# A graph network's edge bucketing: source and destination packed into one 16-bit value, shorter sums, slot rows written in two halves

## What is computed

```python
def _layernorm(x, axis=-1, eps=1e-05):
    m = jnp.mean(x, axis=axis, keepdims=True)
    v = jnp.var(x, axis=axis, keepdims=True)
    return (x - m) / jnp.sqrt(v + eps)
...
# layer 0: attention over the edges; each edge (rows, cols) = (src, dst)
def _L0_gnn_ref(embeds, qW, kW, vW, rows, cols):
    q = (embeds[rows] @ qW).reshape(e, HEADS, dh)
    k = (embeds[cols] @ kW).reshape(e, HEADS, dh)
    v = (embeds[cols] @ vW).reshape(e, HEADS, dh)
    scores = jnp.clip(jnp.einsum('ehd,ehd->eh', q, k), -10.0, 10.0)
    exp_s = jnp.exp(scores)
    norms = jax.ops.segment_sum(exp_s, rows, num_segments=nvar)[rows]
    w = exp_s / (norms + 1e-08)
    res = jax.ops.segment_sum(w[:, :, None] * v, rows, num_segments=nvar).reshape(nvar, d)
    return embeds + res
...
h = jnp.maximum(_layernorm(x, axis=-1), 0.0)
x = x + _L0_gnn_ref(h, L0_gnn_qW, L0_gnn_kW, L0_gnn_vW, src, dst)
h = jnp.maximum(_layernorm(x, axis=-1), 0.0)
x = x + _L1_gnn_ref(h, src, dst, L1_gnn_W, L1_gnn_b)      # softmax-weighted sum over incoming edges, linear
h = jnp.maximum(_layernorm(x, axis=-1), 0.0)
x = x + _L2_gnn_ref(h, edge_index)                        # ten normalized propagation steps
h = jnp.maximum(_layernorm(x, axis=-1), 0.0)
x = x + _L3_gnn_ref(h, edge_index, L3_gnn_W1, L3_gnn_b1, L3_gnn_W2, L3_gnn_b2)  # two graph convolutions
return x
```

## Time and profile before

| | us |
|---|---|
| median of 3 runs | 4279.61 |
| the profiled execution | 4284.03 |
| its span, first to last instruction | 4282.7 |
| bucketing loop, from the first `bt` to the last copy of placed values | 61.96 to 310.2 |
| from there to the landing of the first row load of attention | 310.2 to 329.8 |
| busy over the whole span: TensorE / VectorE / ScalarE / GpSimd | 3994 / 1952 / 1447 / 602 |

### The profile page before, as it was taken

The page is one execution under the profiler, slowest core; times in us unless marked ns, Lnnn a source line. Parts: engine busy times, 40 slices in busy tenths (PEclk is TensorE's granted clock), DMA queues, the critical chain, the costliest instruction groups (busy, mean ns, idle before and its releaser), DMA issues.

```text
span 4282.7 us, 126097 instructions
## 1 busy us (share of the span) xinstructions
PE 3994.3 (93%) x46462; PEld 3761.0 (88%) x46462; DVE 1951.5 (46%) x4496; ACT 1446.9 (34%) x4588; POOL 601.5 (14%) x707
## 2 busy tenths in 40 slices
PE   2668999999997999899999999999999999979898
PEld 2558999999995556699999999999999999979898
DVE  8998999999997233322222222222222222251211
ACT  1226777777776010122222222222222222221100
POOL 1004656665652000000000000000000000000000
PEclk9778999999998999999999999999999999989899
DMA  1004455455454333256566565655565556546574
GB/s 38 2 4 148 157 169 168 153 173 164 153 172 147 108 112 104 106 202 204 202 202 203 202 204 202 204 201 204 200 205 201 204 200 205 199 147 207 163 214 138
DMA packets 304056, 705.71 MB, mean 165 GB/s; under 512 B 32571, under 2 KB 228539, under 8 KB 303928
## 3 DMA queue, kind: packets, MB, share of 16 engines
q1 hardware_dynamic: 299542, 703.17, 50.6%
q10 hardware_dynamic: 4386, 0.73, 0.1%
HBM read 620.51 MB, written 83.32 MB: 164 GB/s over the span
## 4 chain that ended last, share of the span: by engine, by line
PE 74%; DVE 11%; issue 6%; POOL 4%; DMA 2%; ACT 1%; DVEq 0%; SPq 0%; ACTq 0%; POOLq 0%
PE sum L1544 46%; PE sum L1289 14%; PE sum3a L1289 4%; PE pk L1059 3%; POOL sc L1011 2%; PE pr L1081 2%; POOL wv L1016 2%; DVE onerank L738 1%; DMA rows<-slot_rows_d 1%; DVE qk L935 1%; PE pq L1071 1%; DVE sc L942 1%; DVE hd L983 1%; DVE hT L954 1%; DVE bt L701 1%
## 5 line engine op out<-in xcount | busy, mean ns | idle before, releaser
L1544 PE MATMUL sum<-y,ring 128*128 128x192 f16 x12005 | 993.9, 246 | 4.9 <-ACT y L1446 4.9
L1544 PEld LDWEIGHTS sum<-y,ring 128*128 128x128 fp8e4 x12005 | 992.8, 98 | 5.4 <-issue 5.1
L1544 PE MATMUL sum<-u2b,ring 128*128 128x192 f16 x12005 | 991.2, 246 | 0.0
L1544 PEld LDWEIGHTS sum<-u2b,ring 128*128 128x128 fp8e4 x12005 | 990.5, 98 | 0.0
L1289 PE MATMUL sum<-u,ring 128*128 128x385 f16 (+1 forms) x4802 | 613.0, 288 | 31.1 <-ACT u L1414 22.2
L1552 DVE TENSOR_TENSOR z<-lo,sum 128x96 f32<-128x96 f32 x490 | 124.8, 255 | 1118.8 <-ACT lo L1567 1117.9
L1289 PEld LDWEIGHTS sum<-u,ring 128*128 128x128 fp8e4 x4802 | 435.7, 98 | 198.9 <-issue 36.7
L1059 PE MATMUL pk<-kv,hT 128*128 128x192 f16 x4900 | 488.3, 247 | 22.6 <-DVE hT L954 15.8
L1059 PEld LDWEIGHTS pk<-kv,hT 128*128 128x128 f16 x4900 | 408.8, 99 | 30.6 <-DVE hT L954 15.2
L1144 ACT ACTIVATE kvs<-pk 128x384 f32<-128x384 f32 x735 | 309.0, 437 | 204.9 <-PE pk L1059 139.9
L1567 ACT ACTIVATE lo<-sum 128x96 f32<-128x96 f32 x490 | 123.2, 251 | 745.7 <-PE sum L1544 745.7
(11 more groups left out here) (247 smaller groups left out, 3693.1 us busy)
## 6 DMA issues: line engine op xcount, KB each, us to landing
ring<-adjacency_t SPq DMA_DIRECT2D x490, 800.0 KB, 4.3
ring<-adjacency SPq DMA_DIRECT2D x147, 896.0 KB, 5.0
rows<-slot_rows_d SPq DMA_DIRECT2D x245, 320.0 KB, 6.4
adjacency<-row SPq DMA_DIRECT2D x49, 800.0 KB, 3.4
adjacency_t<-col SPq DMA_DIRECT2D x49, 800.0 KB, 6.0
out_dram<-X SPq DMA_DIRECT2D x6, 336.0 KB
slot_rows_d<-slot_rows SPq DMA_DIRECT2D x4, 156.2 KB
ed<-in_dst_dram ACTq DMA_DIRECT2D x25, 18.0 KB, 1.6
```

What stands on the lines that cost most here:

```text
L1544: m = pe.matmul(ps[r][:, 0:2 * D], w[:, t // 2, :, t % 2], U[:, t, 0:2 * D], start=t == 0, stop=t == TILES - 1)
```

## The change

Source place (0 to 127) and destination place (0 to 255) of an edge go into one 16-bit word, read as bfloat16: the source in the low 7 bits, where its fraction lies, 64 plus the destination's low 7 bits in the exponent, and the destination's eighth bit as the sign (`code`). A product with the one-hot matrix and a sum over zeros keep such a value as it is, so one `vals` of 49 columns takes the place of two. `same2`, `same4` and `prod4` are no longer made: `tensor_rank` adds 36 rows of `same`, which is now in two buffers, the 49th tile, and 24 columns of `prod2`. After the loop VectorE takes the bits apart again in two halves of the tiles (24 and 26), in uint16, into values in float16 that are transposed; ScalarE issues two of the first half's four row writes, SP the others, and the second half's four. Only the first half's are waited for at the end of bucketing; the second half's before attention loads its fifth chunk. The planes of `slots` are uint16 with other codes for the high part, and `hT` is compared with numbers that begin at 64 for the destination (`dpid`, one more iota on GpSimd at the start). ScalarE computes one exponent at the end of bucketing (`warm`). The diff, cut to its core:

```diff
+FIRST_D = 64
+HALF_X = 12
...
+        code = k.buf(ctx, "code", [P, GROUPS, RUN], U16)
...
-        vals = [k.buf(ctx, f"vals{i}", [P, TWOS_RUN, 2, TILES, 2], BF16) for i in range(2)]
+        vals = [k.buf(ctx, f"vals{i}", [P, TWOS_RUN, TILES, 2], BF16) for i in range(2)]
...
-        prod4 = k.buf(ctx, "prod4", [P, TWOS_RUN, EVEN // 4, 2], BF16)
-        same = k.buf(ctx, "sameb", [P, 2, TWOS_RUN, RUN], BF16)
-        same2 = k.buf(ctx, "same2", [P, TWOS_RUN, RUN], BF16)
-        same4 = k.buf(ctx, "same4", [P, RUN // 4, RUN], BF16)
+        same = [k.buf(ctx, f"sameb{i}", [P, 2 * TWOS_RUN, RUN], BF16) for i in range(2)]
...
+        placed = k.buf(ctx, "placed", [P, BTILES, GROUPS], BF16)
+        rows16 = k.buf(ctx, "rows16", [P, 2, BTILES, GROUPS], F16)
+        identh = k.buf(ctx, "identh", [P, P], F16)
+        warm = k.buf(ctx, "warm", [P, 1], F32)
...
+        x_halves = ((0, HALF_X), (HALF_X, PAIRS))
+        pt = [projection.turned[:].bitcast(F16)] + [projection.out[:, i, :].bitcast(F16) for i in range(2)]
...
+            v.tensor_copy(identh[:], k.ident[:])
+            v.memset(placed[:, TILES:BTILES, :], 0.0)
             v.wait_ge(k.base1.sem, k.base1.at(2))
             v.tensor_tensor(rel[:], k.ed[:], over(base[:], RUN), ALU.subtract).then_inc(k.prepared.sem, 1)
             v.tensor_scalar(ti[:], k.es[:], 7, None, ALU.logical_shift_right).then_inc(k.prepared.sem, 1)
+            v.tensor_scalar(half_d, k.ed[:], P, 8, ALU.bitwise_and, ALU.logical_shift_left)
             projection.roots()
             v.wait_ge(k.prepared.sem, k.prepared.at(1))
             v.tensor_scalar(valid[:], rel[:], float(GROUP - 1), None, ALU.is_le).then_inc(k.prepared.sem, 1)
-            v.tensor_scalar(dloc[:], rel[:], 1.0, None, ALU.add)
+            v.tensor_scalar(lower, k.ed[:], P - 1, 7, ALU.bitwise_and, ALU.logical_shift_left).then_inc(k.prepared.sem, 1)
             v.wait_ge(k.prepared.sem, k.prepared.at(3))
             v.scalar_tensor_tensor(valid[:], rel[:], 0.0, valid[:], ALU.is_ge, ALU.mult).then_inc(k.prepared.sem, 1)
+            v.wait_ge(k.prepared.sem, k.prepared.at(2))
+            v.tensor_scalar(k.es[:], k.es[:], P - 1, None, ALU.bitwise_and).then_inc(k.prepared.sem, 1)
             projection.units()
-            v.wait_ge(k.prepared.sem, k.prepared.at(4))
+            v.wait_ge(k.prepared.sem, k.prepared.at(6))
             v.scalar_tensor_tensor(tile1, ti[:], 1.0, valid[:], ALU.add, ALU.mult).then_inc(k.prepared.sem, 1)
-            v.wait_ge(k.prepared.sem, k.prepared.at(5))
-            v.tensor_scalar(ti[:], k.es[:], P - 1, None, ALU.bitwise_and).then_inc(k.prepared.sem, 1)
+            v.scalar_tensor_tensor(lower, lower, float(FIRST_D * P), k.es[:], ALU.add, ALU.add).then_inc(k.prepared.sem, 1)
+            v.wait_ge(k.prepared.sem, k.prepared.at(7))
             v.tensor_copy(tile_odd[:, :, 0:2 * RUN - 1], tile0[:, :, 1:2 * RUN]).then_inc(k.prepared.sem, 1)
-            v.wait_ge(k.prepared.sem, k.prepared.at(6))
-            v.tensor_scalar(sloc[:], ti[:], 1.0, None, ALU.add).then_inc(k.prepared.sem, 1)
             v.wait_ge(k.prepared.sem, k.prepared.at(8))
+            v.tensor_tensor(code[:], lower, half_d, ALU.add).then_inc(k.prepared.sem, 1)
+            v.wait_ge(k.prepared.sem, k.prepared.at(10))
...
+            for h, (x0, x1) in enumerate(x_halves):
+                t = slice(2 * x0, 2 * x1)
+                bits = placed[:, t, :].bitcast(U16)
+                v.tensor_scalar(filled[:, t, :], bits, 0.5, None, ALU.is_gt, ALU.add,
+                                accum_out=k.full[:, h:h + 1]).then_inc(k.full_s.sem, 1)
+                v.tensor_scalar(place[:, t, :], bits, P - 1, None, ALU.bitwise_and).then_inc(k.codes.sem, 1)
+                v.tensor_scalar(second[:, t, :], bits, 2.0 ** 15 - 0.5, 256.0, ALU.is_gt, ALU.mult).then_inc(k.codes.sem, 1)
+                v.tensor_scalar(exponent[:, t, :], bits, 7, None, ALU.logical_shift_right).then_inc(k.codes.sem, 1)
+                v.wait_ge(k.full_s.sem, k.full_s.at(h + 1))
+                v.wait_ge(k.codes.sem, k.codes.at(3 * h + 1))
+                v.scalar_tensor_tensor(rows16[:, 0, t, :], place[:, t, :], 1.0, filled[:, t, :], ALU.add,
+                                       ALU.mult).then_inc(k.decoded.sem, 1)
+                v.wait_ge(k.codes.sem, k.codes.at(3 * h + 3))
+                v.scalar_tensor_tensor(rows16[:, 1, t, :], second[:, t, :], -0.5, exponent[:, t, :], ALU.mult,
+                                       ALU.add).then_inc(k.decoded.sem, 1)
+            bits = placed[:].bitcast(U16)
+            v.scalar_tensor_tensor(k.slots[:, 0, :, :], place, 1.0, filled[:], ALU.add, ALU.mult).then_inc(k.planes.sem, 1)
+            v.tensor_scalar(k.slots[:, 2, :, :], second[:], 1.0, None, ALU.max).then_inc(k.planes.sem, 1)
+            v.tensor_scalar(k.slots[:, 1, :, :], bits, 11, HIGH_D - 1, ALU.logical_shift_right,
+                            ALU.bitwise_and).then_inc(k.planes.sem, 1)
+            v.tensor_scalar(k.slots[:, 3, :, :], bits, 7, LOW_D - 1, ALU.logical_shift_right,
+                            ALU.bitwise_and).then_inc(k.planes.sem, 1)
             v.wait_ge(k.full_ps.sem, k.full_ps.at(1))
-            v.tensor_copy(k.filled[:], pc[0:1, 0:1]).then_inc(k.filled_s.sem, 1)
+            v.tensor_reduce(k.filled[:], pc[0:1, 0:2], AX.X, ALU.add).then_inc(k.filled_s.sem, 1)
...
+            if g >= 2:
+                v.wait_ge(k.ranked.sem, k.ranked.at(g - 1))
             for odd, t in enumerate((tile0, tile_odd)):
-                v.tensor_tensor(same[:, odd, :, :], under(tile1[:, g, :], TWOS_RUN), moved(t, g),
-                                ALU.is_equal).then_inc(k.same.sem, 1)
+                v.tensor_tensor(same[i][:, odd * TWOS_RUN:(odd + 1) * TWOS_RUN, :], under(tile1[:, g, :], TWOS_RUN),
+                                moved(t, g), ALU.is_equal).then_inc(k.same.sem, 1)
             v.wait_ge(k.bt.sem, k.bt.at(g + 1))
             if g >= 2:
                 v.wait_ge(k.placed.sem, k.placed.at(g - 1))
-            v.tensor_tensor(vals[i][:, :, 0, :, :], bt[i][:], of_group(sloc, g), ALU.mult).then_inc(k.sval.sem, 1)
-            v.wait_ge(k.same.sem, k.same.at(4 * g + 2))
-            v.tensor_tensor(same2[:], same[:, 0, :, :], same[:, 1, :, :], ALU.add).then_inc(k.same.sem, 1)
-            v.tensor_tensor(vals[i][:, :, 1, :, :], bt[i][:], of_group(dloc, g), ALU.mult).then_inc(k.dval.sem, 1)
-            v.wait_ge(k.same.sem, k.same.at(4 * g + 3))
-            if g:
-                v.wait_ge(k.ranked.sem, k.ranked.at(g))
-            v.tensor_tensor(same4[:], same2[:, 0:RUN // 4, :], same2[:, RUN // 4:, :], ALU.add).then_inc(k.same.sem, 1)
+            v.tensor_tensor(vals[i][:], bt[i][:], of_group(code[:].bitcast(BF16), g), ALU.mult).then_inc(k.val.sem, 1)
...
-            v.wait_ge(k.prod.sem, k.prod.at(3 * g + 2))
-            v.tensor_tensor(prod4[:], prod2[:, :, 0:EVEN // 4, :], prod2[:, :, EVEN // 4:, :], ALU.add).then_inc(k.prod.sem, 1)
...
-            pe.wait_ge(k.slots_out.sem, k.slots_out.at(GROUPS))
-            for n in range(2 * PAIRS):
-                i, x = divmod(n, PAIRS)
+            for n, (h, i, x) in enumerate((h, i, x) for h, (x0, x1) in enumerate(x_halves) for i in range(2)
+                                          for x in range(x0, x1)):
+                if n in (0, 2 * HALF_X):
+                    pe.wait_ge(k.decoded.sem, k.decoded.at(2 * h + 2))
                 if n >= 24 and n % 8 == 0:
                     pe.wait_ge(k.rows_sb.sem, k.rows_sb.at(n // 8 - 2))
                 pe.transpose(pt[n // 8 % 3][0:2 * GROUPS, (n % 8) * P:(n % 8 + 1) * P],
-                             flat(k.slots[:, i, 2 * x:2 * x + 2, :]), k.identb[:]).then_inc(k.rows_t.sem, 1)
-            pe.wait_ge(k.full_s.sem, k.full_s.at(1))
-            pe.matmul(pc[0:1, 0:1], k.ones[:, 0:1], k.full[:], start=True, stop=True).then_inc(k.full_ps.sem, 1)
+                             flat(rows16[:, i, 2 * x:2 * x + 2, :]), identh[:]).then_inc(k.rows_t.sem, 1)
+            pe.wait_ge(k.full_s.sem, k.full_s.at(2))
+            pe.matmul(pc[0:1, 0:2], k.ones[:, 0:1], k.full[:], start=True, stop=True).then_inc(k.full_ps.sem, 1)
...
-            parts = [same4[:, j, :].rearrange("p (a t) -> p a t", t=2) for j in range(RUN // 4)]
-            parts += [prod[:, :, j, :] for j in range(EVEN, TILES)] + [prod4[:, :, j, :] for j in range(EVEN // 4)]
+            parts = [same[g % 2][:, j, :].rearrange("p (a t) -> p a t", t=2) for j in range(RUN)]
+            parts += [prod[:, :, j, :] for j in range(EVEN, TILES)] + [prod2[:, :, j, :] for j in range(EVEN // 2)]
...
-                t = pe.matmul(po[:, 0:2 * TILES], onerank[:, r // 2, :, r % 2],
-                              vals[g % 2][:, r // 2, :, :, r % 2].rearrange("p i k -> p (i k)"), start=r == 0, stop=r == RUN - 1)
+                t = pe.matmul(po[:, 0:TILES], onerank[:, r // 2, :, r % 2], vals[g % 2][:, r // 2, :, r % 2],
```

(59 more changed lines are left out.)

53 lines of the change are left out of this document (19 added, 34 removed).

## The result

The kernel after took 4226.98 us in the median of 4 runs (4226.25 to 4227.45), the kernel before 4279.34 in 4 runs beside it (4278.96 to 4280.45): a ratio of 0.9877, interval 0.986 to 0.9894, or 52.4 us less. The forecast was 4230.7, in a range of 4224 to 4246. The profiled execution of after took 4226.87, at the median of its runs; that of before took 4284.03, 4.4 above its own.

What follows compares the result with a forecast made beforehand. VectorE was taken to bound the bucketing loop. Codes +2.0, loop -48.0, slot rows in halves -1.6 and exp table -1.3 sum to -48.9 us, from 4279.6 to 4230.7, range 4224 to 4246.

Steps and rivals of the forecast that it cites:

- likeliest case: Whole kernel: bucketing turns of 7.7 to 8.05 us, giving 4226 to 4237 us; chance 0.69.
- Preparation: Ahead of the bucketing loop: making the codes adds 2.0 us on VectorE, bounds +1.4 to +3.
- First and last turn: Bucketing loop's ends: first turn 3.0 us shorter, last turn 0.6 longer as no VectorE bucketing work hides rank.
- placing: Behind the last turn: 12 placing matmuls of half the width and a copy of 49 elements save 1.0 us.
- The turn: Bucketing loop: a turn falls from 9.80 to 7.86 us, 44.6 us less over 23 turns.
- Rank: TensorE in each bucketing turn: 61 matmuls instead of 22, 2.10 us at low clock, 1.86 at high.
- Codes and halves: Between bucketing and attention: 3.0 us of decoding, then slot rows written in halves; net -1.6 us, bounds +2 and -3.5.
- Exp table: Start of attention: loading the table earlier, while slot rows are written, saves the load's 1.28 us, counted as -1.3.
- Attention: Attention's 49 copies of uint16 slots, 100 elements each: 0 us more, bound 2.5.
- (a): Bucketing loop: TensorE takes over the turn, 8.2 to 8.6 us each, total 4238 to 4248 us; chance 0.26.
- (b): Bucketing loop: the burst of 61 rank matmuls becomes the bound, making the kernel slower, 4294 us; chance 0.02.
- (c): Bucketing loop: VectorE's saving moves into waits on `before` or ScalarE's copies, total 4271 to 4288 us; chance 0.02.

Runs made afterwards that it cites:

- 85 rank matmuls: The kernel after with `prod2` not made either, its sums left to TensorE: 4215.96 us, ratio 0.9849 to the kernel before.
- one run: The kernel before with the early exponent alone added: 4277.10 us, ratio 0.9989 to the kernel before.
- the other: The kernel after with a copy in place of the early exponent, so the table load is back in attention: 4233.35 us, ratio 0.9886 to the kernel before.

## Why the prediction was right

The time came 3.7 below the forecast and inside its likeliest case. Step by step:

- **Preparation.** +2.0 forecast, +1.75 measured. The f16 identity cost nothing as said: its cast takes 1.56 us beside GpSimd's memset, and `rel` starts at 53.24 (53.38 before).
- **First and last turn.** -3.0 and -3.02; +0.6 and +0.73; placing -1.0 and -1.00.
- **The turn.** 7.86 forecast, 7.751 measured, so that 23 turns gave 47.2 in place of 44.6. This term was mis-sized. VectorE's own steps, 7.78, were right to 0.03; what was wrong is the 0.1 for rank coming late, and the mean clock behind it ("the projection averages nearer its low price"). I carried the 0.76 of before into the new kernel. In the stretch it became 0.94, and rank came late in none of the 23 turns. I had priced a turn at the low level from the last placing matmuls to rank (rank starts at 5.3, the next `onerank` at 7.9); in the six turns that touch the low level these matmuls still ran at 1.00, and in the closest one rank starts at 5.05 and just fits (`rankb` done at 157.54, `onerank` at 157.58). My price for the full low turn was met by no turn, so no run tests it. The thin margin itself was real: with 85 rank matmuls rank sets the turn, even at a clock of 1.00, at 7.176, where VectorE's own is 7.109.
- **Rank.** 1.86 and 2.10 forecast, 2.04 and 2.25 measured, 0.2 above. The `same` parts take 25 ns each at the high level and 31 at the low one, less than the 30.5 and 34.5 carried over, but those of `prod2` 46 ns at both levels (busy 1.29 at 162.93 with the clock at 1.00, 1.28 at 178.66 with it at 0.50). The stationary strides in the placing matmuls cost nothing: the last third of 12 takes 0.33 us at the high level (152.57 to 152.90), 28 ns each, not 81. At the low level it takes 0.51 in the kernel with the small sums back (157.28 to 157.79), 43 ns each; the 41 that I took was for that level.
- **Codes and halves.** Decoding 3.0 forecast, 2.93 measured; row load at T + 13.7, as forecast; its landing at T + 17.5 against about 18.0. -1.6 forecast, -2.1 measured. The run with late writes splits it into +2.9 and -5.0.
- **Exp table.** -1.3 forecast, -4.9 in the profiles, about -4 to -6 in medians (3.9 by one run, 4.8 to 5.8 by the other). The direction was right, the size a quarter of it. The step that failed is "I count the load alone": the load sat ahead of the first weighing, TensorE ran dry, and then ran some 6 us at the low level. Of 5.3 us counted from the same matmuls, 2.4 are the longer pause and 2.9 TensorE's clock, which I never looked at there.
- **Attention.** 0 forecast for reading uint16 slots, +0.24 in 48 tiles between these two traces. But the 48 tiles take 957.60 to 960.10 us in the three traces with bf16 slots and 959.18 to 961.48 in the seven with uint16, so a cost of 1 or 2 us is neither shown nor excluded.
- **Rivals.** (a), a turn of 8.2 to 8.6, was excluded by 7.751; its condition, 81 ns for a placing matmul, was 28 to 43. (b) needed 66 ns for a rank matmul; the dearest took 46. The figure of 81 ns in the Trainium skill ("TensorE: Matmul & The Clock Gate", Back-to-back issue gap) is for 128 columns, and the runs show 25 to 46 ns with 36. (c) needed a new wait; `onerank` waits in none of the 23 turns.

The -48.9 of the sum and the -57.2 between the profiles thus differ by 2.6 in the turn, 3.6 in the exponent, 0.5 in the halves and 1.6 in stages that weren't touched; the small rest is spread over the other steps. Of the medians, 4.8 less is seen. So part of the closeness is luck: all told the terms fell 8.3 us short of what the two traces differ by, and had the medians differed by 57.2 too, the time would have been 4222, below my range. Open is why the profiled execution of before lies 4.4 above its own median. The fills differ from trace to trace by 2.1 us with the late load (25.59 to 27.67) and by 1.1 without it, which is too little by itself, and an execution without a profile doesn't show its fill.
